# Attention with layer norm over 16 images of 900 tokens: value and output tiles of 128 tokens, the last four tokens of all images in shared tiles

## The reference

```python
x_seq = x.reshape(16, 900, 512)                       # B images, 30 x 30 tokens, d = 512
q, k, v = (x_seq @ w + b, split into 8 heads of 64)   # for wq, wk, wv
scores = einsum('bhqd,bhkd->bhqk', q, k) / 8 + bias   # bias by Manhattan distance of the tokens
attn = softmax(scores)
ctx = einsum('bhqk,bhkd->bhqd', attn, v)              # back to (B, 900, 512)
resid = ctx @ wo + bo + x_seq
out = (resid - mean) * rsqrt(var + 1e-5) * gamma + beta    # layer norm over the 512 features
```

## Time and profile before

| | us |
|---|---|
| timed runs, median of 3 | 3186.41 (3181.86 to 3192.68) |
| profiled execution, time | 3174.42 |
| profiled execution, span from first to last instruction | 3172.5 |
| PE busy in the span | 3027.3 (95%) |
| ACT busy | 2709.9 (85%) |
| DVE busy | 2649.1 (84%) |
| POOL busy | 1615.2 (51%) |
| mean granted PE clock | 0.991 of full speed |

### The profile page before, as it was taken

The page is one execution under the profiler, slowest core; times in us unless marked ns, Lnnn a source line. Parts: engine busy times, 40 slices in busy tenths (PEclk is TensorE's granted clock), DMA queues, the critical chain, the costliest instruction groups (busy, mean ns, idle before and its releaser), DMA issues.

```text
span 3172.5 us, 111090 instructions
## 1 busy us (share of the span) xinstructions
PE 3027.3 (95%) x44584; PEld 2073.6 (65%) x44584; DVE 2649.1 (84%) x5594; ACT 2709.9 (85%) x6839; POOL 1615.2 (51%) x3277
## 2 busy tenths in 40 slices
PE   7999999999999999999999999999999999999986
PEld 5666666666666666666666666666666666666654
DVE  3878889798897978879798897988979788797887
ACT  4988898888989888898888988888898898988885
POOL 1346445464553745546464454645536455464643
PEclk9999999999999999999999999999999999999998
DMA  7332423324243342323324233241433423233221
GB/s 206 72 82 73 99 63 95 81 71 109 57 97 85 78 98 68 86 78 92 88 73 102 60 95 84 76 104 54 97 82 78 102 69 90 74 91 89 73 66 28
DMA packets 523228, 266.81 MB, mean 84 GB/s; under 512 B 329274, under 2 KB 460346, under 8 KB 522590
## 3 DMA queue, kind: packets, MB, share of 16 engines
q1 hardware_dynamic: 375479, 127.82, 18.3%
q10 hardware_dynamic: 147232, 131.88, 14.1%
HBM read 194.10 MB, written 63.44 MB: 81 GB/s over the span
## 4 chain that ended last, share of the span: by engine, by line
PE 47%; DVE 15%; ACT 14%; SPq 11%; DMA 6%; issue 5%; POOL 2%; ACTq 0%; DVEq 0%
PE r_ps L603 13%; PE pv_ps L702 13%; PE s_ps L684 12%; ACT prob L803 7%; PE r_ps L645 6%; ACT prob L819 5%; SPq L496 5%; SPq L486 5%; DVE prob L966 5%; DVE prob_t L982 5%; DMA other<-own 4%; PE r_ps L619 3%; DVE stats L998 2%; DVE tokens L996 1%; DMA v_dram<-stage 1%
## 5 line engine op out<-in xcount | busy, mean ns | idle before, releaser
L803 ACT ACTIVATE prob<-prob,own 128x450 f32<-128x450 f32 x1920 | 1265.3, 662 | 142.3 <-DVE own L966 127.1
L966 DVE CUSTOM_DVE_ANT_0 prob<-s_ps,window 128x450 f32<-128x450 f32 x1920 | 1121.9, 621 | 286.1 <-PE s_ps L684 206.4
L982 DVE STREAM_TRANSPOSE prob_t<-prob 128x960 f32<-128x960 f32 x960 | 1126.6, 1174 | 140.1 <-ACT prob L819 139.8
L819 ACT ACTIVATE prob<-prob,weight 128x450 f32<-128x450 f32 x1920 | 1173.2, 660 | 52.8 <-POOL weight L1113 51.1
L684 PE MATMUL s_ps<-k_sb,q_sb 64*32 64x450 f32 x15360 | 856.4, 548 | 42.9 <-DVE own L966 39.9
L702 PEld LDWEIGHTS pv_ps<-prob_t,values 64*64 64x64 f32 x23040 | 730.0, 133 | 152.8 <-issue 80.1
L702 PE MATMUL pv_ps<-prob_t,values 64*64 64x150 f32 x23040 | 783.6, 290 | 8.5 <-DVE prob_t L982 8.4
L603 PE MATMUL r_ps<-xt,w_sb 128*128 128x450 f32 x3072 | 686.1, 373 | 27.5 <-ACT k_sb L760 13.5
L603 PEld LDWEIGHTS r_ps<-xt,w_sb 128*128 128x128 f32 x3072 | 572.1, 190 | 172.8 <-issue 69.8
L1099 POOL TENSOR_TENSOR lead<-own,other 128x4 f32<-128x4 f32 x480 | 96.6, 201 | 925.9 <-DMA other<-own 924.4
L1113 POOL TENSOR_TENSOR weight<-total,minus_one 128x4 f32<-128x4 f32 x480 | 501.0, 1044 | 37.6
(11 more groups left out here) (63 smaller groups left out, 1475.9 us busy)
## 6 DMA issues: line engine op xcount, KB each, us to landing
w_sb<-w_split ACTq DMA_DIRECT2D x126, 512.0 KB, 3.9
values<-v_dram ACTq DMA_DIRECT2D x256, 240.0 KB, 3.3
other<-own SPq DMA_DIRECT2D x1920, 1.0 KB
tokens<-in_x SPq DMA_DIRECT2D x420, 64.0 KB, 2.6
tokens<-in_x SPq DMA_DIRECT2D x109, 240.0 KB, 3.6
out<-tokens SPq DMA_DIRECT2D x105, 240.0 KB, 2.8
v_dram<-stage SPq DMA_DIRECT2D x90, 240.0 KB, 3.0
v_dram<-stage SPq DMA_DIRECT2D x30, 180.0 KB, 2.3
```

Source lines behind the costliest of these rows:

```text
L803: nc.scalar.activation(prob[:, im.unit(u) % RING, head, 0:HALF], prob[:, im.unit(u) % RING, head, 0:HALF], ACT.Exp, scale=-1.0, bias=own[: ...
L819: nc.scalar.activation(prob[:, im.unit(u) % RING, head, 0:HALF], prob[:, im.unit(u) % RING, head, 0:HALF], ACT.Copy, scale=weight[:, s, c: ...
L966: nc.vector.tensor_tensor_reduce(prob[:, im.unit(u) % RING, head, 0:HALF], s_ps[:, u % 2, head, 0:HALF], window[:, w0:w0 + HALF // GRID, : ...
L982: nc.vector.transpose(out=prob_t[:, g % 2, v % PER_GROUP, :, :].rearrange("p h k -> p (h k)"), in_=prob[:, im.unit(u) % RING, :, :].rearra ...
```

## The change

The tile becomes 128 tokens. Seven full tiles make 896 tokens of an image; the four that are left (REST) of all 16 images make one more tile of 64 rows for values and one for outputs, once in the program instead of once per image.

- The table of gaps loses one output tile (at u = 4) and one value tile (at u = 34 the second one); the values, and the pieces behind them, take new places.
- The rest's values are computed in the prologue from a gathered tile (`first_x(FULL)`, four DMAs), kept in a DRAM buffer `v_rest`, and copied for each image into its place by one DMA on SP (`rest_values`, four rows). The rest's contexts are collected by a small POOL copy per image (`keep_rest`) in `ctx_rest`, and their output tile is the last of the finals, stored by four DMAs.
- The value tile over the boundary of the halves is stored by two DMAs. There are four slots for staged values instead of two (two of them in the context's memory); `x_turned` moves into the memory of `ctx_split`, `ident` into that of `ctx_rest`, and `ratio` and `total` become `lead`.
- The loads of x are issued two DMAs at a time over two bodies. The next residual is loaded one body later. A value tile or a key or query piece of the next image waits only for the x tiles that it reads.

```diff
-TT = 120
-NT = -(-S // TT)
+TT = 128
+FULL = S // TT
+REST = S - FULL * TT
+REST_ROWS = REST * B
+NT = FULL + 1
...
-SPLIT_UNITS = [0, 0, 3, 5, 6, 10, 13, 15]
-LOAD_X = [20, 22, 26, 29]
-X_UNITS = [30, 31, 32, 33, 34, 36, 38, 40]
+SPLIT_UNITS = [0, 0, 3, 5, 9, 13, 15]
+REST_UNIT = 3
+LOAD_X = [20, 24, 28, 26, 31, 33, 35, 37]
+X_UNITS = [30, 31, 33, 35, 37, 39, 41, 42]
+STAGE_SLOT = [0, 1, 2, 3, 0, 1, 0]
...
-FINAL_UNITS = [54, 54, 58, 58, 60, 62, 62, 64]
+FINAL_UNITS = [54, 54, 58, 58, 62, 62, 64, 64]
...
-GAPS = {2: pieces(1, (3,)) + [out(0)], 4: [out(1), out(2)], 8: [out(3)] + pieces(2, (0,)), 12: [out(4)] + pieces(2, (1,)),
+GAPS = {2: [out(0)] + pieces(1, (3,)), 4: [out(1)], 8: [out(2)] + pieces(2, (0,)), 12: [out(3)] + pieces(2, (1,)),
...
         def context_of(t):
+            if t == FULL:
+                return ctx_rest[:, :, :, :].rearrange("p a i b -> p a (i b)")
+            return ctx_sb[:, :, t * TT:t * TT + TT]
...
+            def rest_values(b):
+                sp.wait_ge(v_rest_kept, 16)
+                sp.dma_start(v_dram[b % 2, 1, HALF - REST:HALF, :], v_rest[:, b, :]).then_inc(v_rest_in, 16)
...
-                for work in im.out_tiles(u - 5):
+                for work in im.out_tiles(u - 6):
...
+                        for a in range(128 // QUAD):
+                            if u == LOAD_X[t] + a // 2:
+                                load_x(im.b + 1, t, a)
...
-                if j == 0 and p == PAIRS and im is not pro:
-                    pe.wait_ge(x_lo, X_TILES * (im.b + 1))
+                if p == PAIRS and im is not pro:
+                    pe.wait_ge(x_lo, X_TILES * im.b + x_tiles_to(HALF * (half + 1)))
...
-                    act.wait_ge(v_kept[t % 2], 16 * (NT // 2 * (im.b + 1) + t // 2))
+                    act.wait_ge(v_kept[i], kept_in(i, im.b + 1) + kept_to(i, t))
...
+            def keep_rest(b):
+                pool.wait_ge(ctx_kept, GROUPS * (b + 1))
+                nc.gpsimd.tensor_copy(ctx_rest[:, :, :, b], ctx_sb[:, :, FULL * TT:S]).then_inc(ctx_rest_kept, 1)
```

246 lines of the change are left out of this document (153 added, 93 removed).

## The result

The changed kernel takes 3148.06 us in the median (3145.55 to 3151.23), the kernel before on the same chip 3188.02 (3181.86 to 3192.68). The ratio is 0.9887 with a 95% interval of 0.9864 to 0.9909: faster by 40 us, where 82 were forecast. The profiled executions differ by less, 3174.42 to 3151.23 (3188.02 less 3174.42 is 13.6: that execution of before was quicker than its median, so by the medians some 13 us less are missing than the profiles show).

A forecast was written before the change was run, and what follows sets the result against it. PE, busy 2621.05 of 2699.55 us, was taken as the bound. 14 x (2.3 + 3.5) = 81 us, 87.5 with first and last images, less 2 and 3 gives 82.5: 3186.4 - 82.5 = 3104 us, range 3070 to 3143.

The forecast's parts named there:

- The matmuls that go: Output and value tiles on PE: 30 tiles fewer at 2.88 us each, 86.4 us, with 128 rows costing no more than 120.
- that rival, at 7%: All remaining output and value tiles: 128 rows cost 7% more than 120, taking back 45 us, 3149 us; chance 0.04.
- The first half of an image: Step u = 4: one output tile and two waits go, DVE is late at u = 6 and 8; gains 2.3 us.
- The second half: Steps u = 34 and 44: a value tile and some waits go, 0.5 us lost to thin steps; gains 3.5 us.
- I take 0.5 of the 1.1 us as left: Value tile of u = 34: PE's wait for the x tile shrinks from 1.1 to 0.5 us an image.
- work taken from PE comes off the time until another engine is late: The fourteen images: PE's own work sets the pace, so removing it shortens the time; 2.88 us counted in each half.
- Moved at no cost: Work moved or added on SP, POOL, ACT and DVE costs nothing; DVE loses an output tile, some 3 us an image.
- The ends: First image gains 4 us, last gains 2.3; prologue loses 2 and the tail 3, between 1 and 6.
- DVE and ACT set the pace: Rival in the thinned steps: first half gains only 1.0 us and second 2.3, 3142 us; chance 0.20.
- The exchange comes late by SP: Rival on SP: exchanges queue behind loads waiting for stores, 11.6 us an image, 81 us slower, 3267 us; chance 0.04.
- all waits go: Rival: all of PE's waits go and none comes, 8 us an image, 113 us in all, 3073 us; chance 0.15.
- three signs named beforehand: Prediction wrong if PE waits over 9 us an image, POOL's exchange wait grows, or the tail exceeds 26 us.

The follow-up runs named there:

- out0_behind: Changed kernel with the piece put ahead of output tile 0 at u = 2 again, as before the change: 3152.83 us, ratio 0.9916 to the kernel before.
- pool_order: Changed kernel with GpSimd's split of the x tiles moved ahead of its totals and leads: 3135.56 us, ratio 0.9864 to the kernel before.
- sp_odd: Changed kernel with the first four loads of x one u later (21, 25, 29, 27): 3140.77 us, ratio 0.9868 to the kernel before.
- thin_before: Kernel before with 11 of 12 matmuls left out of output tile 2 and value tile 3 of each image, nothing moved: 3199.4 us, ratio 1.0063.
- pool_copy: Changed kernel with the four exchange DMAs on SyncE replaced by four GpSimd copies, nothing left out: 3037.51 us, ratio 0.9537 to the kernel before.
- before_pool_copy: Kernel before with the four exchange DMAs on SyncE replaced by four GpSimd copies: 3125.04 us, ratio 0.9814 to the untouched kernel before.

## Why the prediction was wrong, point by point

**The matmuls that go** were right. The mean matmul of output and value tiles with 128 rows, in the page of the changed kernel:

```profile
L702 PE MATMUL r_ps<-wo_sb,ctx_split 128*128 128x512 f32 x1356 | 354.6, 412 | 29.4 <-POOL ctx_split L1203 15.1
...
L676 PE MATMUL r_ps<-wv_sb,xt 128*128 128x512 f32 x1344 | 338.5, 401 | 65.0 <-POOL xt L1223 65.0
```

412 and 401 ns, for 405 and 400 in the earlier trace rows with 120 rows, so rows are free within 2% and that rival, at 7%, falls. 30 tiles at 2.88 us were 86.4 us, and the pair without SyncE's exchange differs by 87.5. That it fits so well is in part luck: of the 87.1 us by which its fourteen images differ, 75.4 are PE's busy time and 11.7 its idle time, and without any exchange the pair differs by 97.5. The weight load is 189 ns for values and 193 for outputs, near the 190 taken. The price of the Trainium skill ("TensorE: Matmul & The Clock Gate", "Back-to-back issue gap"), 131 ns a matmul and so 47 us for all, is not borne out by these 87.5. That it is near the 40 measured is chance, since the 40 are the full price less new waiting.

**The first half of an image** had the right mechanism. PE does wait for DVE at u = 6 and 8 (the rows are below, 1.32 and 1.52 us), 2.2 us on the mean over the fourteen images where 3.3 were put. Counted by the starts of DVE's score rows, the scores that PE makes at u = 10 come 2.7 us earlier in an image, where 2.3 were forecast. But of the waits that were to go, that for the split context stayed, 14.0 us for 9.7, since output tile 0 now stands ahead of the piece that had covered it, and that for `q_sb` only moved to the scores, 6.6 for 9.3. out0_behind shows that the first of these costs nothing net.

**The second half** is the step that failed: "The second half gains 2.88 + 0.6 + 0.5 - 0.5 = 3.5 us". By the same count it loses 0.8, since the image as a whole gains 1.9. Without SyncE's exchange it gains 2.7 and the first half 3.5. Of its terms, "I take 0.5 of the 1.1 us as left" was right only for the place it was made for: the value tile of u = 34 waits 0.2 us. The new waits stand at u = 32, 38 and 42, for which the forecast put nothing, and make the wait for x tiles 60.1 / 14 = 4.3 us. The forecast asked how many loads stand ahead of one exchange, found fewer, and stopped there. It also read GpSimd's wait of 3.85 us in the earlier trace rows as lateness by eight loads, but GpSimd waits for an exchange at 339 of the 420 pairs before, 2.3 us each.

pool_order shows that even this wait, once gone, comes back elsewhere, so the step that carries the failure is in the first part: "work taken from PE comes off the time until another engine is late". It was taken to hold for 5.8 us an image and held for 1.9. Each link, 85 and 87% busy, was looked at by itself, and the chain through them, with 5.07 us from the last sum to the lead in it, was not measured. The rows for it could have been had: GpSimd's 784.8 us of waiting for the exchange in the fourteen images, and ScalarE's 76.3 for the leads. What the runs showed in its place is 3.54 us of new idle time an image, which goes when the exchange leaves SyncE. That the exchange is the cause is shown by both pairs; how it works back on each place of PE is argued from the waits.

**Moved at no cost.** SyncE's waits for stores are as forecast, 103.8 us for 97.4. DVE's lost output tile did not show as a gain.

**The ends.** Output tile 0 now stands ahead of a piece of 2.6 us, which is taken off here. The start gained 266.01 - 259.32 - 2.6 = 4.1 us, where 4 less 2 were forecast. The last image lost 2.0 where 2.3 of gain were put, and gains 3.6 in the pair without SyncE's exchange. The tail from the finals to the end grew from 47.1 to 52.3 us, 5.2 where 3 were put, within its bounds of 1 to 6. PE there waits for the rest's split:

```profile
3125.55 7.39 PE L702 MATMUL r_ps<-wo_sb,ctx_split 128*128 128x512 f32 x24 [2.02 <-DVE ctx_split L1094]
```

**The rivals.** "DVE and ACT set the pace", 3142 us at a chance of 0.20, came nearest in time, yet for a reason that it didn't have: neither engine is full, they wait for each other through SyncE. "The exchange comes late by SP" named the right queue at 0.04, and had a price of 11.6 us an image where the new idle time is 3.5. Its cause, loads waiting for stores, is seen in the pair shown above, but it is a small one on the whole: sp_odd moves these loads behind the exchange and gains 6 us. What the forecast lacked is the case between them: the exchange as it is, with nothing new queued ahead of it, too slow for an image of 187 us. Without it the pairs differ by 87.5 and 97.5 us, between the forecast's 82.5 and the 113 of "all waits go". Two of the three signs named beforehand did tell: PE waits 9.15 us an image (over 9), and GpSimd's wait for the exchange grew, 802.5 for 784.8 in a stretch 26 us shorter. The third, the tail behind the last context group, stayed just under its 26 us, with 25.9 (20.6 before).

## What to carry to other kernels

An engine at 97% is the bound only while the chain of the others around it has room: before crediting work taken from it, follow one value through all engines back to where it is needed, add up that chain, issue and landing of its DMAs included, and compare it with the new period. Pair each result with the work that waits for it by its count, not by what stands next to it in time: here the sum nearest ahead of a lead belongs to the next pair. If every wait that is removed shows up under another name, suspect such a chain; leave out one link in both kernels and see whether the difference between them changes. Values of a few bytes for each partition that go to a neighbouring quarter of the partitions were cheaper in both of these kernels as four copies of 32 partitions on an engine with time to spare (0.91 us here) than as four DMAs (2.5 us of issue and the landing behind it).

## What the runs showed of the hardware

**The granted clock falls behind PE's waits, even in kernels whose PE is 95 and 97% busy.** In the fourteen images the changed kernel has four such falls, the kernel before two, thin_before eleven, pool_copy and before_pool_copy none. Here is one, of the changed kernel, as PE in order of time and then as stretches of 5 us (length, PE busy, granted clock, DMA share, GB/s):

```profile
648.37 3.06 PE L702 MATMUL r_ps<-wo_sb,ctx_split 128*128 128x512 f32 x12
...
658.41 0.99 PE L741 MATMUL s_ps<-k_sb,q_sb 64*32 64x450 f32 x16 [1.32 <-DVE own L1042]
660.92 1.38 PE L741 MATMUL s_ps<-k_sb,q_sb 64*32 64x450 f32 x16 [1.52 <-DVE own L1042]
662.23 4.22 PE L702 MATMUL r_ps<-wo_sb,ctx_split 128*128 128x512 f32 x12
```

```profile
655.00:660.00 5.00, 3.08 (x84) 1.00 0.20 52
660.00:665.00 5.00, 4.08 (x23) 0.66 0.18 50
665.00:670.00 5.00, 5.00 (x46) 1.00 0.35 106
```

The two waits are those forecast at u = 6 and 8. Behind them the granted clock is 0.66 in the mean of 5 us, so it was at the lower of its levels, 1.2 and 2.4 GHz, for a part of them, and the output tile takes 4.22 us where the same twelve matmuls took 3.06 a little earlier. By these two rows the fall cost 1.2 us, so the four, some 5 us by that estimate, are a small part of the 42 us that are missing; in thin_before eleven would be some 13. The other three falls stand behind the same two waits of another image, behind one of 2.2 us for an x tile and behind one of 2.0 us for transposed rows. Two waits of 2.7 and 2.6 us for x tiles brought none. The clock was 1.00 in the earlier trace rows and no cost of it was put; the new waits brought a small one.

**PE's busy time falls when the exchange leaves SyncE**, by 11 us over the fourteen images in both kernels (2545.30 to 2534.46, 2621.05 to 2609.86) with the same matmuls. In the changed kernel the falls of the clock are part of that; in the kernel before they are too few to be. That cause is open.
